# Six-stage decoder on one core: weights packed on the host and fetched a stage ahead, one preparation block, shifted rows fetched four batches at a time

## The chip, the cores and the metric

The kernel runs on one core of a Trainium2 chip. The time is the device time of one execution in microseconds (us); the number shown is the median of three runs. A profile is a separate execution, recorded by the hardware profiler, and it has its own time. The engines are PE (matrix products; PEld is its loading of weights), DVE, ACT and POOL (vector, activation and general work on SBUF), and SP, which here only issues DMAs.

## The reference: what is computed

The input is x, 64 batches of 128 tokens with 128 channels (f32), and a context of 64 batches of 77 rows with 64 channels. Two layers are applied, each of three blocks with a residual around it. `ln` is a layer norm without weights.

```python
x = x + linear_attention(ln(x))              # 16 heads of 8, random features, causal
x = x + cross_attention(ln(x), ctx)          # 16 heads of 64, 77 keys
x = x + local_transformer(ln(x))             # two layers, as below
x = x + mamba2(ln(x))                        # two directions, 4-tap convolution, scan over 128 tokens
x = x + context_attention(ln(x), ctx)        # 16 heads of 8
x = x + experts(ln(x))                       # 16 experts, top 2, silu

# one layer of the local transformer
h = shift_token(x)                           # channels 64..127 come from the token before, 0 for the first
q, k, v = split(h @ wqkv)                    # 8 heads of 64, normed, rotary position
x = x + local_attention(q, k, v) @ wo        # window of 64 tokens
h = layernorm(shift_token(x)) * ln_g + ln_b
a, g = split(h @ w1 + b1)                    # 341 columns each
x = x + (a * gelu(g)) @ w2 + b2
```

`shift_token` is the operation that a part of the change is about. Tokens lie on the 128 partitions, so to shift by a token is to move rows from partition p to p + 1. The kernel does it with two DMAs from SBUF to SBUF: channels 0 to 63 of 128 rows unmoved, and channels 64 to 127 of 127 rows moved down by one.

## The kernel before

The residual stream lives in SBUF (`k_x`, [128 tokens, 64 batches, 128 channels]). The stages run one after another. Each is one block with one instruction stream per engine, and each stream is a software pipeline over the 64 batches (`pipeline`, L99): step n of an engine's stream handles phase 0 of batch n, phase 1 of batch n-1 and so on, in an order that is written out by hand in its `step` function. Semaphores (`Stage`, L77) say which instruction of which batch another engine has finished. `at("c", b, ago=2)` is a wait for the instruction "c" of two batches back, as when a buffer of a pair is used again.

At the end of a stage `Memory.free` (L127) clears its semaphores and meets all engines at a barrier. SBUF buffers are allocated by stage, so nothing of a stage can be started before the last one is over. Each stage therefore begins with its weights' DMAs on SP's queue, small ones among them (one row spread over all partitions, one column), and the other engines wait on the semaphore `loaded` for all of them.

The stages, with the prefix of their names in the trace, are:

- constants (`k_`, L161), a block for POOL alone: identity, masks;
- linear attention (`la_`, L215): 30 weight DMAs, then x per batch;
- cross attention (`ca_`, L616), ahead of it a block `cw_` that loads four weight arrays, transposes them on PE and multiplies Wq with Wk and Wv with Wo head by head;
- local attention (`l_`, L996) and gated MLP (`m_`, L1345), twice. `lt_y` is the stream inside, `lt_hn` (`g.hn`) the shifted copy of it. Local attention's SP stream fetches the shifted rows of each batch for its own use (`l_h`, L1092 and L1093) and, once the batch's result is added to y, fetches the shifted rows of the result into `lt_hn` (L1083 and L1084). The block ends with SP waiting for all of these. POOL clears row 0 of `lt_hn` first (L1104). The gated MLP works on quads, four batches at a time: 16 quads in a pipeline of five phases, STAT, NORM, TURN, GATE, OUT. DVE takes statistics of the quad in `lt_hn` (L1549), POOL subtracts and scales (L1422, L1426), PE turns the quad into columns (L1513), DVE scales it into `m_hT` (L1567), and PE multiplies with w1 (L1484) and w2 (L1492);
- state model (`mb_`, L1587), ahead of it a block `mw_` that loads its arrays, multiplies the input projection with each of the four convolution taps on DVE, transposes and multiplies on PE;
- context attention (`xa_`, L2149) and experts (`mo_`, L2462). The experts' stage writes x out.

DVE's stream in the gated MLP matters for the prediction. In a step its phases come in the order STAT of quad n, GATE of quad n-3, OUT of quad n-4, TURN of quad n-2. So the first `m_hT`, that of quad 0, stands in step 2 behind the statistics of quad 2.

## Time and profile before

| | |
|---|---|
| time, median of 3 runs | 4214.08 us (4212.66 to 4217.06) |
| the profiled execution | 4216.15 us, span 4214.3 us |
| PE busy | 3899.9 us, 93% |
| PE's weight loads | 3022.5 us, 72% |
| DVE busy | 3020.9 us, 72% |
| ACT busy | 2842.6 us, 67% |
| POOL busy | 1818.1 us, 43% |
| TensorE clock granted, mean | 0.975 |

PE by fortieths of the span (a digit is the busy share in tenths, a slice is 105 us):

```profile
PE   6999799999979999788999986999999989998999
```

The span is that of all engines from the first instruction to the last; 1.85 us of the execution lie outside it. Where the digit falls to 6 or 7, two stages meet inside the slice, or (slices 12, 17 and 18) the local attention waits for other engines. In the timeline `SPq` is SP's queue of DMA issues; the length beside one is the issue, not the transfer. In the windows, "PEclk" is the share of full clock that was granted to TensorE in the stretch, "share" the mean busy share of the 16 DMA engines.

### The profile page before, as it was taken

The page shows a single profiled execution, that of the slowest core. Times are in us where ns is not written, and L with a number is a line of the kernel's source. Part 1 is how long each engine was busy: PE and PEld are TensorE (multiplying, and loading weights), DVE is VectorE, ACT ScalarE, POOL GpSimd, SP SyncE. Part 2 cuts the span into 40 slices and gives each one's busy share as a digit, 9 for nine tenths or more (in the row PEclk, how much of TensorE's full clock was granted, in tenths as well). Part 3 has the DMA queues.
Part 4 walks back from the last instruction along what each step waited for, and adds up shares of the span by engine and source line. Part 5 has one row for each costly group of instructions (what it writes and reads, how often), then busy time and mean ns, then how long its engine had stood idle before and what let it go on. Part 6 is the DMA issues. An engine that isn't in the chain of part 4 may idle for free. (4 is left out here: it accounts for less than half of the span.)

```text
span 4214.3 us, 107514 instructions
## 1 busy us (share of the span) xinstructions
PE 3899.9 (93%) x34047; PEld 3022.5 (72%) x34047; DVE 3020.9 (72%) x7623; ACT 2842.6 (67%) x6414; POOL 1818.1 (43%) x1728
## 2 busy tenths in 40 slices
PE   6999799999979999788999986999999989998999
PEld 4676678888746666675666675888888867776777
DVE  6888655555569999548999854777777757775665
ACT  5666455555569999648999963777777757774333
POOL 3333122222268888536777752333333321112443
PEclk9999899999989999999999998999999989999999
DMA  0000000000000000000000000000000000000000
GB/s 16 9 9 9 19 9 6 6 6 6 5 23 17 16 16 16 12 14 14 16 17 16 14 8 15 1 0 0 0 0 0 0 6 4 3 3 20 12 12 13
DMA packets 129425, 40.97 MB, mean 10 GB/s; under 512 B 104042, under 2 KB 128428, under 8 KB 129324
## 3 DMA queue, kind: packets, MB, share of 16 engines
q1 hardware_dynamic: 129324, 39.67, 4.0%
q8 instruction: 58, 0.95, 0.1%
q14 instruction: 43, 0.35, 0.0%
HBM read 18.72 MB, written 4.19 MB: 5 GB/s over the span
## 5 line engine op out<-in xcount | busy, mean ns | idle before, releaser
L1139 POOL TENSOR_TENSOR l_rc<-l_rc,l_rs 128x1024 f32<-128x1024 f32 x128 | 303.6, 2372 | 202.9 <-DVE l_rs L1332 201.2
L1206 ACT ACTIVATE l_prob<-l_prob,l_mx 128x128 f32<-128x128 f32 x1024 | 311.9, 389 | 0.0
L1824 POOL TENSOR_TENSOR mb_steps<-mb_upto,mb_dta 128x1024 f32<-128x1024 f32 x64 | 121.4, 1897 | 361.0 <-DVE mb_dta L2075 361.0
L780 POOL TENSOR_TENSOR ca_prob<-ca_prob,ca_sm 128x1232 f32<-128x1232 f32 x64 | 143.9, 2248 | 299.7 <-DVE ca_sm L946 299.7
L1231 PE MATMUL l_qk_ps<-l_wqkv,l_hT 128*128 128x512 f32 x512 | 248.6, 609 | 12.4 <-DVE l_rs L1332 10.4
L1133 POOL TENSOR_TENSOR l_prob<-l_prob,l_sm 128x1024 f32<-128x1024 f32 x128 | 242.8, 1897 | 17.1 <-DVE l_sm L1318 17.1
L1116 POOL TENSOR_TENSOR l_rc<-l_rc,l_ss 128x1024 f32<-128x1024 f32 x128 | 243.4, 1902 | 12.5 <-POOL l_rc L1139 4.5
L1976 PE MATMUL mb_x_ps<-mb_wx,mb_xT 128*128 128x256 f32 x1024 | 237.5, 386 | 0.0
L2548 POOL TENSOR_TENSOR mo_hid<-mo_hid,mo_gate 128x1024 f32<-128x1024 f32 x64 | 121.7, 1902 | 199.9 <-DVE mo_hid L2694 199.9
L1327 DVE TENSOR_REDUCE l_ss<-l_sq 128x16 f32<-128x1024 f32 x128 | 156.0, 1219 | 72.1 <-ACT l_sq L1170 71.8
L1976 PEld LDWEIGHTS mb_x_ps<-mb_wx,mb_xT 128*128 128x128 f32 x1024 | 190.8, 191 | 23.0
L1239 PEld LDWEIGHTS l_att_ps<-l_probT,l_val 128*64 128x64 f32 x2048 | 109.2, 136 | 127.4 <-ACT l_probT L1157 127.4
L2025 DVE SCALAR_TENSOR_TENSOR mb_pre<-mb_bc_ps,mb_cw,mb_pre 128x127 f32<-128x127 f32 (+2 forms) x576 | 193.1, 345 | 1.6 <-ACT mb_pre L1871 1.6
L807 ACT ACTIVATE ca_oT<-ca_go_ps 128x1024 f32<-128x1024 f32 x64 | 65.5, 1024 | 190.2 <-PE ca_go_ps L860 190.2
L1484 PE MATMUL m_ag_ps<-m_hT,m_w 128*128 128x256 f32 (+1 forms) x768 | 181.4, 388 | 1.9 <-DVE m_hT L1567 1.9
L2245 POOL TENSOR_TENSOR xa_kblock<-xa_kT,xa_gmask 128x308 f32<-128x308 f32 x64 | 44.8, 700 | 293.0 <-ACT xa_kT L2285 293.0
L1268 PEld LDWEIGHTS l_score_ps<-l_kT,l_qT 64*128 64x128 f32 x2048 | 124.6, 188 | 64.8 <-issue 51.7
L1296 DVE TENSOR_TENSOR l_prob<-l_score_ps,k_local 128x1024 f32<-128x1024 f32 x128 | 156.0, 1218 | 14.7 <-PE l_score_ps L1268 11.0
L1239 PE MATMUL l_att_ps<-l_probT,l_val 128*64 128x128 f32 x2048 | 140.1, 279 | 26.2 <-ACT l_probT L1157 9.7
L2579 ACT ACTIVATE mo_hidT<-mo_turn_ps 128x512 f32<-128x512 f32 x128 | 69.5, 594 | 139.6 <-PE mo_turn_ps L2623 139.6
L1315 DVE TENSOR_REDUCE l_sm<-l_prob 128x8 f32<-128x1024 f32 x128 | 155.5, 1215 | 8.1 <-ACT l_prob L1206 3.8
L958 DVE TENSOR_TENSOR k_x<-k_x,ca_y_ps 128x128 f32 (+1 forms) x64 | 18.4, 287 | 193.8 <-PE ca_y_ps L896 193.8
(377 smaller groups left out, 12208.5 us busy)
## 6 DMA issues: line engine op xcount, KB each, us to landing
la_xin<-in_x SPq DMA_DIRECT2D x64, 64.0 KB
l_h<-lt_y SPq DMA_DIRECT2D x128, 32.0 KB
lt_hn<-lt_y SPq DMA_DIRECT2D x128, 32.0 KB
out_x<-k_x SPq DMA_DIRECT2D x64, 64.0 KB, 1.5
l_h<-lt_y SPq DMA_DIRECT2D x128, 31.8 KB
lt_hn<-lt_y SPq DMA_DIRECT2D x128, 31.8 KB
ca_ctxT<-in_ctx_T SPq DMA_DIRECT2D x128, 19.2 KB, 2.0
l_wqkv<-in_L_ffn_wqkv SPq DMA_DIRECT2D x2, 768.0 KB
```

What stands on the lines that cost most here:

```text
L1116: gp.tensor_tensor(rc[l][:].rearrange("p a h e -> p (a h) e"), rc[l][:].rearrange("p a h e -> p (a h) e"), ss[l][:, 2].unsqueeze(2).to_bro ...
L1133: gp.tensor_tensor(heads, heads, sm[b.lane][:, 1].unsqueeze(2).to_broadcast([T, H, T]), ALU.mult).then_inc(*pool_prob.did("norm"))
L1139: gp.tensor_tensor(wide(rc[l][:]), wide(rc[l][:]), wide(rs[l][:]), ALU.add).then_inc(*pool_sum.did("rot"))
L1206: ex = sc.activation(p[:, a, j], p[:, a, j], ACT.Exp, bias=mx[l][:, a, j:j + 1])
L1231: mm = te.matmul(qk_ps[:, a], hT[b.slot][:], wqkv[:, a], start=True, stop=True)
L1239: mm = te.matmul(att_ps[HD * a:HD * a + HD, j], val[b.slot][:, 2 * j + a], probT[l][:, a, j], start=True, stop=True)
L1296: v.tensor_tensor(prob[b.slot][:].rearrange("p a j t -> p (a j) t"), score_ps[:].rearrange("p a j t -> p (a j) t"), g.local[:].unsqueeze(1 ...
L1315: v.tensor_reduce(sm[l][:, 0], prob[b.slot][:].rearrange("p a j t -> p (a j) t"), AX, ALU.add).then_inc(*vec_sum.did("sum"))
L1327: v.tensor_reduce(ss[l][:, 0], sq[l][:].rearrange("p a h e -> p (a h) e"), AX, ALU.add).then_inc(*vec_rot.did("ss"))
L1484: mm = te.matmul(ag_ps[half][0:M[c], c, N * a:N * a + N], w1[:, a, 128 * c:128 * c + M[c]], hT[b.lane][:, N * half:N * half + N], start=Tr ...
L1976: mm = te.matmul(x_ps[:, DI * k:DI * k + DI], xT[l][:, at_j:at_j + T], wx[:, k, j], start=(j == 0), stop=(j == TAPS - 1))
L2025: v.scalar_tensor_tensor(out=out, in0=bc_ps[:, T * i + there.start:T * i + there.stop], scalar=cw[:, k, 2 + SHIFTED[i][1], TAPS - 1 - back ...
```

## The change

Four things are changed.

*Packed weights.* The host lays the weights of each stage out as one array of 128 rows, with rows spread over partitions, columns and padding already in place (`laid_out`, `packed`). `Memory.weights` allocates the buffer and gives views by name. The sizes are 1284 columns for the linear attention (657 KB), 3072 for the cross attention, 2565 and 700 for the state model, 2304 and 1202 for each layer of local attention and gated MLP (1.80 MB a layer), 642 for the context attention and 3232 for the experts (1.98 MB together).

*Fetched a stage ahead.* These buffers outlive the stages, and one semaphore `g.fetched` counts all of them. SP issues the loads of the cross attention and the state model behind the last input of the linear attention, those of both local layers behind the last context of the cross attention, and those of the last two stages at the beginning of the state model. The constants are made by POOL inside the linear attention's block.

*One preparation block.* `prepare` stands between linear and cross attention and holds the work of `cw_` and `mw_`. ACT, not DVE, copies the cross products out of PSUM; POOL makes the scan's masks and the diagonal of D. The block `mw_` in front of the state model is gone.

*Shifted rows by quads.* `lt_hn` is gone. Local attention issues only its own fetches and waits for nothing at its end. The gated MLP's SP stream, empty before but for weights, fetches the shifted rows of a quad with two DMAs (128x4x64 and 127x4x64) into a pair of buffers `m_h`, in the phase STAT. A fetch waits until POOL has read the quad two back.

```diff
     def free(self):
-        self.nc.clear_and_free_semaphores(self.sems)
-        self.nc.all_engine_barrier()
+        if self.sems:
+            self.nc.clear_and_free_semaphores(self.sems)
+            self.nc.all_engine_barrier()
...
+    def weights(self, name, key):
+
+        buf = self.sb(name, [128, sum(width for _, width in PACKED[key])])
+        parts, start = {}, 0
+        for part, width in PACKED[key]:
+            parts[part] = buf[:, start:start + width]
+            start += width
+        return buf, parts
...
 # linear attention, SP
-                sp.dma_start(wqkv[:], d["L0_attn_Wqkv"]).then_inc(loaded, 16)
...
+                sp.dma_start(w[:], d["p_linear"]).then_inc(loaded, 16)
...
                 pipeline(sp, g.NB, LAST + 2, step, turn=4)
+                sp.dma_start(g.cross_w[:], d["p_cross"]).then_inc(g.fetched, 16)
+                sp.dma_start(g.state_w[:], d["p_state"]).then_inc(g.fetched, 16)
+                sp.dma_start(g.steps_w[:], d["p_steps"]).then_inc(g.fetched, 16)
+                sp.dma_start(g.cross_bo[:], row_bc(d["L0_xattn_bo"])).then_inc(g.fetched, 16)
...
 # cross attention, SP
                 pipeline(sp, g.NB, OUT + 1, step, turn=4)
+                for layer in (0, 1):
+                    sp.dma_start(g.local_w[layer][0][:], d["p_local"][layer]).then_inc(g.fetched, 16)
+                    sp.dma_start(g.gated_w[layer][0][:], d["p_gated"][layer]).then_inc(g.fetched, 16)
+                sp.dma_start(g.rot[:], d["rot"]).then_inc(g.fetched, 16)
...
 # local attention, SP
-                    b = at(OUT)
-                    if b:
...
-                        sp.wait_ge(*vec_y.at("y", b))
-                        sp.dma_start(to_low, low).then_inc(hn_in, 16)
-                        sp.dma_start(to_high, high).then_inc(hn_in, 16)
...
-                sp.wait_ge(hn_in, 32 * g.NB)
...
 # local attention, POOL
-                gp.memset(g.hn[0:1, :, HALF:C], 0.0).then_inc(zeroed, 1)
...
 # gated MLP, SP
                 sp.wait_ge(zeroed, NZERO)
-                sp.dma_start(lng[:], d["L0_ffn_ln_g"][layer].unsqueeze(1)).then_inc(loaded, 16)
...
+                def step(at):
+                    b = at(STAT)
+                    if b:
+                        index = b.index * Q if b.trip is None else sp.snap(b.index * Q)
+                        low = g.y[:, bass.ds(index, Q), 0:HALF]
+                        high = g.y[0:T - 1, bass.ds(index, Q), HALF:C]
+                        sp.wait_ge(*pool_norm.at("c", b, ago=2))
+                        sp.dma_start(h[b.lane][:, :, 0:HALF], low).then_inc(h_in[b.lane], 16)
+                        sp.dma_start(h[b.lane][1:T, :, HALF:C], high).then_inc(h_in[b.lane], 16)
+
+                pipeline(sp, g.NB // Q, OUT + 1, step)
...
 # gated MLP, POOL
                 for l in (0, 1):
+                    gp.memset(h[l][:], 0.0).then_inc(zeroed, 1)
...
-                        gp.tensor_tensor(off[l][:], quad(g.hn, b), mv[l][:, :, 0].unsqueeze(2).to_broadcast([T, Q, C]),
+                        gp.tensor_tensor(off[l][:], h[l][:], mv[l][:, :, 0].unsqueeze(2).to_broadcast([T, Q, C]),
...
 # gated MLP, DVE
+                        v.wait_ge(h_in[l], b.loaded(32))
                         for i in range(Q):
-                            v.bn_stats(stats[l][:, i], one(g.hn, b, i)).then_inc(*vec_stat.did(f"s{i}"))
+                            v.bn_stats(stats[l][:, i], h[l][:, i]).then_inc(*vec_stat.did(f"s{i}"))
```

The PE stream of the new block, with its own waits (`turned`, `copied`, `product`, `done` belong to the cross weights, `tap`, `across`, `kept` to the state model's):

```python
te.wait_ge(g.fetched, NFETCH)
for j in range(PAIRS):                      # 8 transposes of wq, then 16 of wk and wv
    mm = te.transpose(pc[:, j // 4, C * (j % 4):C * (j % 4) + C], wq[:, 128 * j:128 * j + 128], g.ident[:])
...
taps(0)                                     # 10 transposes of direction 0, tapped on DVE
te.wait_ge(copied, 3)
...                                         # 16 products for wqk
te.wait_ge(kept, NKEPT[0])
taps(1)                                     # 13 transposes of direction 1
...                                         # 16 products for wvo
```

Behind them come eight transposes and eight products for the state model's wz, wdt and wout.

The order of instructions at three places. On SP, where the cross attention ends and the local attention begins, there stand before (semaphores have the name that they were first given, so those of a later stage read `la_...`):

```order
92 L746 UNCONDITIONAL_BRANCH
93 L1059 UNCONDITIONAL_BRANCH [waits barrier_Pool_Activation_PE_DVE_SP_release]
94 L1061 DMA l_wqkv<-in_L_ffn_wqkv 128x1536
95 L1062 DMA l_wo<-in_L_ffn_wo 128x4x128
96 L1065 DMA l_qks<-in_L_ffn_q_scale 128x64
97 L1066 DMA l_qks<-in_L_ffn_q_scale 128x32
98 L1067 DMA l_qks<-in_L_ffn_q_scale 128x32
99 L1065 DMA l_qks<-in_L_ffn_k_scale 128x64
100 L1066 DMA l_qks<-in_L_ffn_k_scale 128x32
101 L1067 DMA l_qks<-in_L_ffn_k_scale 128x32
102 L1068 DMA l_rot<-in_rot 128x256
103 L1092 DMA l_h<-lt_y 128x64 [waits la_pe_last,la_zeroed]
```

And of the change:

```order
74 L680 DMA ca_ctx<-in_ctx 77x64 [waits la_act_feat] x4
75 L684 DMA w_local<-in_p_local 128x2304
76 L685 DMA w_gated<-in_p_gated 128x1202
77 L684 DMA w_local<-in_p_local 128x2304
78 L685 DMA w_gated<-in_p_gated 128x1202
79 L686 DMA w_rot<-in_rot 128x256
80 L662 UNCONDITIONAL_BRANCH
81 L1060 UNCONDITIONAL_BRANCH [waits barrier_Pool_Activation_PE_DVE_SP_release]
82 L1076 DMA l_h<-lt_y 128x64 [waits la_pe_score1,la_loaded]
```

The loads have moved across the barrier, into the cross attention's block, and hold for both layers; the first fetch of shifted rows is now the first thing that SP does in the local attention.

On DVE, in the first steps of the gated MLP, the statistics of quads 1 and 2 and the first `m_hT` stand before as:

```order
645 L1549 BN_STATS m_stats<-lt_hn 128x6 [waits la_act_keyT]
646 L1549 BN_STATS m_stats<-lt_hn 128x6 x3
647 L1551 MEMSET m_rstd 128x4 [waits la_prep]
648 L1553 BN_AGGR m_mv<-m_stats 128x2 x4
649 L1549 BN_STATS m_stats<-lt_hn 128x6 [waits la_act_keyT]
650 L1549 BN_STATS m_stats<-lt_hn 128x6 x3
651 L1551 MEMSET m_rstd 128x4 [waits la_prep]
652 L1553 BN_AGGR m_mv<-m_stats 128x2 x4
653 L1567 TENSOR_SCALAR m_hT<-m_turn_ps,m_lng,m_lnb 128x512 [waits la_act_turn,la_vec_last,la_loaded]
```

And of the change:

```order
657 L1532 BN_STATS m_stats<-m_h 128x6 [waits la_prep,la_act_keyT]
658 L1532 BN_STATS m_stats<-m_h 128x6 x3
659 L1534 MEMSET m_rstd 128x4 [waits la_made]
660 L1536 BN_AGGR m_mv<-m_stats 128x2 x4
661 L1532 BN_STATS m_stats<-m_h 128x6 [waits la_zeroed,la_act_keyT]
662 L1532 BN_STATS m_stats<-m_h 128x6 x3
663 L1534 MEMSET m_rstd 128x4 [waits la_made]
664 L1536 BN_AGGR m_mv<-m_stats 128x2 x4
665 L1547 TENSOR_SCALAR m_hT<-m_turn_ps,w_gated 128x512 [waits la_act_turn,la_vec_last]
```

The order is the same. Each group of statistics now has a second semaphore to wait for (`la_prep` and `la_zeroed` are the two lanes of `h_in`), that of the quad's fetch, and the first `m_hT` stands behind that of quad 2.

On SP the gated MLP's block of the change begins with

```order
130 L1373 UNCONDITIONAL_BRANCH [waits barrier_Pool_Activation_PE_DVE_SP_release]
131 L1384 DMA m_h<-lt_y 128x4x64 [waits la_act_keyT,la_loaded]
132 L1385 DMA m_h<-lt_y 127x4x64
133 L1384 DMA m_h<-lt_y 128x4x64 [waits la_act_keyT]
134 L1385 DMA m_h<-lt_y 127x4x64
135 L1384 DMA m_h<-lt_y 128x4x64 [waits la_act_keyT]
136 L1385 DMA m_h<-lt_y 127x4x64
```

where before it held the gated MLP's weights and no shifted rows.

## Rows read from the trace of the kernel before

**Rows 1.** windows: us, PE PEld DVE ACT POOL busy (x), PEclk, share, GB/s

```profile
0.00:23.05 23.05, 0.00 (x0) 0.00 (x1) 2.03 (x16) 3.56 (x7) 6.20 (x30) 1.00 0.14 30
...
501.45:528.05 26.60, 11.15 (x88) 10.11 (x88) 7.54 (x14) 1.78 (x3) 0.10 (x1) 0.58 0.24 62
...
1165.44:1182.88 17.44, 0.00 (x1) 0.00 (x0) 2.01 (x11) 2.17 (x5) 5.48 (x11) 0.57 0.29 82
...
1730.22:1743.80 13.58, 0.00 (x0) 0.01 (x1) 3.91 (x28) 6.59 (x9) 5.13 (x10) 0.66 0.22 49
...
1743.80:1882.51 138.71, 136.81 (x832) 119.97 (x832) 77.45 (x260) 80.64 (x152) 49.14 (x45) 0.97 0.00 0
...
1882.51:1893.60 11.09, 0.00 (x1) 0.02 (x1) 0.85 (x2) 1.28 (x1) 3.92 (x7) 0.60 0.45 128
...
2430.57:2444.30 13.73, 0.00 (x0) 0.02 (x1) 3.90 (x28) 6.75 (x9) 5.29 (x10) 0.63 0.24 49
...
2582.54:2624.70 42.16, 9.04 (x40) 7.55 (x40) 14.75 (x58) 2.69 (x7) 2.04 (x10) 0.60 0.17 37
...
3421.16:3431.87 10.71, 0.00 (x1) 0.03 (x1) 1.75 (x8) 2.45 (x6) 2.58 (x12) 0.63 0.15 35
```

**Rows 2.** timeline: start, us, engine line op out<-in xcount [idle before <-releaser]

```profile
17.26 0.17 DVE L527 TENSOR_SCALAR la_freq<-la_freq 128x2 f32<-128x2 f32 x1 [17.26 <-DMA la_omega<-in_L_attn_omega]
```

**Rows 3.** windows of the load ahead of the first weight block

```profile
504.00:506.00 2.00, 0.00 (x0) 0.00 (x0) 0.00 (x0) 0.00 (x0) 0.00 (x0) 0.50 0.94 338
...
508.00:510.00 2.00, 0.00 (x0) 0.00 (x0) 0.00 (x0) 0.00 (x0) 0.00 (x0) 0.50 0.89 205
```

**Rows 4.** timeline, first weight block

```profile
510.43 1.97 PE L656 MATMUL cw_pw<-k_ident,cw_wq 128*128 128x128 f32 x8 [8.99 <-DMA cw_wo<-in_L_xattn_Wo]
...
515.08 3.68 PE L667 MATMUL cw_pp<-cw_wkT,cw_wqT 64*128 64x64 f32 x32 [0.78 <-DVE cw_wvT L688]
```

**Rows 5.** timeline, opening of the state model's stage

```profile
2621.62 0.36 POOL L1799 MEMSET mb_xT<- 128x134 f32 x2 [35.71 <-POOLq L127]
```

**Rows 6.** timeline, end of cross-attention and start of local attention

```profile
1122.05 26.66 SPq L765 DMA_DIRECT2D ca_ctx<-in_ctx  x4
...
1166.61 0.36 SPq L1061 DMA_DIRECT2D l_wqkv<-in_L_ffn_wqkv  x1
...
1175.97 0.43 DVE L1287 TENSOR_TENSOR l_rot<-l_rot,l_qks 128x256 f32<-128x256 f32 x1 [10.21 <-DMA l_rot<-in_rot]
```

**Rows 7.** timeline, from local attention into the first gated stage

```profile
1731.15 0.65 SPq L1084 DMA_DIRECT2D lt_hn<-lt_y  x1
...
1735.57 0.10 POOL L1409 MEMSET m_eps<- 128x1 f32 x1 [10.47 <-POOLq L127]
...
1737.05 0.87 DVE L1549 BATCH_NORM_STATS2 m_stats<-lt_hn 128x6 f32<-128x128 f32 x4 [6.51 <-POOL m_gl L1413]
...
1745.00 0.81 DVE L1567 TENSOR_SCALAR m_hT<-m_turn_ps,m_lng,m_lnb 128x512 f32<-128x512 f32 x1 [2.53 <-issue]
...
1745.87 0.80 PE L1484 MATMUL m_ag_ps<-m_hT,m_w 128*128 128x256 f32 x1 [0.96 <-DVE m_hT L1567]
```

**Rows 8.** windows in which one hn half is in transfer (128 rows, 127 rows)

```profile
1731.75:1732.00 0.25, 0.00 (x0) 0.00 (x0) 0.00 (x0) 0.00 (x0) 0.00 (x0) 1.00 0.59 130
...
1732.75:1734.25 1.50, 0.00 (x0) 0.00 (x0) 0.00 (x0) 0.00 (x0) 0.00 (x0) 1.00 0.08 18
```

**Rows 9.** timeline, steady state of the first gated stage, DVE

```profile
1862.59 0.81 DVE L1567 TENSOR_SCALAR m_hT<-m_turn_ps,m_lng,m_lnb 128x512 f32<-128x512 f32 x1 [2.19 <-issue]
...
1870.88 0.81 DVE L1567 TENSOR_SCALAR m_hT<-m_turn_ps,m_lng,m_lnb 128x512 f32<-128x512 f32 x1 [2.18 <-issue]
```

**Rows 10.** timeline, second local layer, SP

```profile
1888.17 0.53 SPq L1092 DMA_DIRECT2D l_h<-lt_y  x1
```

**Rows 11.** timeline, starts of the last two stages, DVE

```profile
3430.12 0.18 DVE L2399 TENSOR_REDUCE xa_gmask<-xa_hmask 128x4 f32<-128x16 f32 x1 [7.66 <-DMA xa_bo<-in_L_xattn_bo]
...
3856.55 0.29 DVE L2648 BATCH_NORM_STATS2 mo_stats<-k_x 128x6 f32<-128x128 f32 x1 [10.03 <-DMA mo_b<-in_L_ffn_b]
```

More of the change, by code:

```diff
@@ L2710, in decoder @@
     with ExitStack() as scope:
[L2711 removed]
+        shared = Memory(nc, scope, "st")
+        g.stored, g.fetched = shared.sem("stored"), shared.sem("fetched")
+        g.NLOCAL, g.NLAST = 9 * 16, 11 * 16
         constants(nc, g, scope)
[L2713 to L2714 removed]
+        kept = Memory(nc, scope, "w")
+        g.rot = kept.sb("rot", [T, 2, 2, ROT_DIM])
+        g.local_w = [kept.weights(f"local{layer}", "local") for layer in (0, 1)]
+        g.gated_w = [kept.weights(f"gated{layer}", "gated") for layer in (0, 1)]
+        g.steps_w, g.steps_part = kept.weights("steps", "steps")
+        g.wx, g.wbc = kept.sb("wx", [C, 2, 4, 256]), kept.sb("wbc", [C, 2, 4, 2, 128])
+        g.wz, g.wdt, g.wout = kept.sb("wz", [C, 2, 2, 128]), kept.sb("wdt", [C, 8]), kept.sb("wout", [128, 2, 2, C])
+        g.ddiag = kept.sb("ddiag", [T, 8, T])
+        g.beyond, g.upto = kept.sb("beyond", [T, 2, T]), kept.sb("upto", [T, 2, T])
+        with ExitStack() as early:
+            cross = Memory(nc, early, "wc", "right")
+            g.wqk, g.wvo = cross.sb("wqk", [C, 8, 2, 64]), cross.sb("wvo", [128, 8, C])
+            g.cross_bo = cross.sb("bo", [T, C])
+            with ExitStack() as once:
+                raw = Memory(nc, once, "wr", "right")
+                g.cross_w, g.cross_part = raw.weights("cross", "cross")
+                g.state_w, g.state_part = raw.weights("state", "state")
+                linear_attention(nc, g)
+                prepare(nc, g)
+            cross_attention(nc, g)
+        local_transformer(nc, g)
+        with ExitStack() as late:
+            last = Memory(nc, late, "wl", "right")
+            g.context_w, g.context_part = last.weights("context", "context")
+            g.experts_w, g.experts_part = last.weights("experts", "experts")
+            mamba(nc, g)
+            context_attention(nc, g)
+            experts(nc, g)
 def kernel(**inputs):
@@ L2721 @@
     nc = bacc.Bacc("TRN2", target_bir_lowering=False, num_devices=1)
-    arrays = {name: np.ascontiguousarray(a) for name, a in inputs.items()}
+    arrays = {name: np.ascontiguousarray(inputs[name]) for name in ("x", "ctx_512", "L0_xattn_bo")}
     arrays.update(shape_tables())
```

684 lines of the change are left out of this document (326 added, 358 removed).

## The prediction

> **What bounds the kernel now.** The page's busy times come first: PE is the busiest engine by far. The windows by stage come next and say where it is not: inside a stage PE hardly stops (136.81 of 138.71 us in the first gated stage), but between stages it does nothing for 11 to 17 us, and at the start and around the two weight blocks the windows are 23, 27 and 42 us long [rows 1]. The change leaves the matmuls of the stages as they are, so its worth lies in these gaps. For each I look in the timeline for the wait that ends last, and for how far behind it PE's first instruction comes.
>
> **Start of the program.** DVE L527 waits until 17.26 for some 30 small loads [rows 2]; PE starts at 23.05 [rows 1], 5.8 later. Afterwards there is one load of 128x1284 numbers (657 KB), issued in the first microsecond. Bulk loads run at 205 to 338 GB/s [rows 3]: 1.9 to 3.2, and 1.4 to 2 from issue to transfer (the gated stage, below, shows 1.4): it lands at 3.9 to 6, I take 5.2. POOL's constants now lie inside the stage; all 30 POOL instructions of that window take 6.20 [rows 1], and I count 5.4 for those that are left ahead of the norm. PE then starts at 5.4 + 5.8 = 11.2: **-12** (-10 to -13).
>
> **First preparation block.** In the 26.60 us ahead of the cross-attention [rows 1] PE L656 waits 8.99 for the load [rows 4]. That goes: the arrays are asked for while the last batches of the linear attention run. In exchange the state model's products, until now a block of their own, are added. At the half clock of this window (0.58 granted [rows 1]) a transpose takes 1.97 / 8 = 0.246 and 32 passes of the products 3.68 [rows 4]. PE's row is then: 24 transposes for the cross weights 4.0 (eight of them, then sixteen with half the columns), taps of direction 0 (10) 2.5, 32 passes 3.7, taps of direction 1 (13) 3.2, 32 passes 3.7, 8 transposes 2.0, 8 products 2.0; 21.1 in all. Waits between engines add some 0.3 and DVE's last scaling 1.1. The state model's first matmul comes 3.1 behind its block's opening (2621.62 [rows 5] to 2624.70 [rows 1]), barrier included 3.8 behind the last instruction; here the chain is one norm shorter: 3.0. From 502.7 that is 502.7 + 21.1 + 1.4 + 3.0 = 528.2, no gain at half clock. With the clock up from the middle of the block (PE now works on without the copies' pauses) it is 5 less, at the full clock from the first transpose 8 less. I take **-3** (-8 to +1).
>
> **Cross-attention to the first local layer.** The cross-attention's last SP instruction is at 1122.05 + 26.66 = 1148.7, the next block opens at 1166.61 [rows 6]. In between now go 3.72 MB (two local, two gated arrays, the table): 11.0 to 18.2 at the rates of rows 3, so they land between 1161.1 and 1168.3, by the middle at 1164. DVE L1287, which waited until 1175.97 for nine loads [rows 6], goes at 1166.9. PE keeps its distance of 6.9 from it (its window ends at 1182.88 [rows 1]), since norm, fetch of h and landing lie between: 1173.85. **-9** (-7 to -9.1).
>
> **Inside local attention** two DMAs a batch and 3.5 us of POOL's fill go. SP isn't waited for in the body and PE's waits there don't name POOL's start: 0.
>
> **Into the gated stage.** Here is the change's price. Before, the last hn fetch is issued at 1731.15, POOL opens the block at 1735.57 once it has landed, DVE's statistics are at 1737.05, the first hT at 1745.00 and the first gate matmul at 1745.87 [rows 7]. DVE's last instruction of the layer ends at 1737.05 - 6.51 = 1730.54. Afterwards the block opens 0.8 behind it, 1731.4 (4.2 earlier), POOL fills for 2.1 (1.5 before), and SP issues the first quad's halves at 1733.5 and 1734.1. What does a quad cost? The old pair shows it: the 128-row half moves at share 0.59 and 130 GB/s, the 127-row half at share 0.08 and 18 GB/s, about one engine of 16 [rows 8]. The quad's 127x4x64 half has 130 KB, 7.2 to 7.4 at 18 GB/s, with the low half's share 7.8. All go through that one engine: with 1.4 to the start and 0.35 to the end's being seen they land at 1743.2, 1751.0, 1758.8, 1766.6. DVE's order puts the third quad's statistics ahead of the first hT (listing in the section on the change), so hT(0) waits until 1758.8 and four statistics (0.87), aggregates (0.4) and hT itself (0.8) follow: the first gate matmul at 1760.9, not 1745.87: **+15.0**.
> In the steady state PE takes a quad each 8.29 (1862.59 to 1870.88 [rows 9]) and the fetch 7.8: PE's body stays, with 0.5 to spare. A fetch waits until POOL has read the buffer of two quads back, some 4 behind that quad's landing and so well inside the 7.8 of the next: the engine doesn't run dry.
> Bounds of this term: if all 16 engines shared the half it would land 2.5 behind the issue; the third fetch is issued once POOL has read the first quad, at about 1741, and hT(0) comes at 1745.5: 0. If four engines shared it, +2.5. Above: 10 per quad would add 16 x 1.7 = 27, and 2.2 for each of three quads at the start.
> The Trainium skill ("DMA: Bandwidth & Descriptors", section "Why a DMA increments its semaphore by 16 and not by 1") has a rule for this: the hardware queue takes the largest number of engines up to 16 that divides the slowest dimension of both patterns, so 127 partitions go on one, 128 on all. The two shares agree with it. By that rule the four batches in the middle don't help, and it speaks against this change; if the whole count 127 x 4 decided, four engines would share the half and the term would be +2.5.
>
> **Second layer.** Into it: POOL and SP open at 1883.84 and SP reaches h's fetch at 1888.17 behind nine loads [rows 10]; now 0.7 after the opening. PE's 1893.60 [rows 1] becomes about 1888.7: **-4.9** (-4 to -5.5; SP no longer waits for the queue either). Its own gated stage has the same waits and the same shape: **+14.9**.
>
> **Into the state model.** Of 42.16 us [rows 1], loads and products last until POOL L1799 at 2621.62 [rows 5]; both go. The block opens at 2583.9 and PE comes 3.1 behind it, 2587.1: **-37.6** (-36 to -40).
>
> **Last two stages.** DVE L2399 comes at 3430.12 after an idle of 7.66, for loads alone [rows 11]; POOL's masks let it go at 3426.05: **-4.1**. DVE L2648 comes at 3856.55 after 10.03 idle [rows 11]; with no load it comes 1.2 after the last stage's end, -8.8, and 0.3 comes back since ACT's table load of 1.28 is then on the way: **-8.5**.
>
> **Sum.** -12 - 3 - 9 + 15.0 - 4.9 + 14.9 - 37.6 - 4.1 - 8.5 = -49.2. Against the profiled execution's own 4216.15 us that is 4167.0. It ran 2.07 over the median shown (4214.08), so the median should be 4165.
>
> **The rivals.**
> (A) The quad's high half spreads over several engines. Then the two +15 become 0 to +2.5 each: 4165 - 25 = 4140, to 4135. For it: the trace holds no transfer of 127 rows with a middle dimension. Against it: the steady 0.08 of the flat one. 15%.
> (B) The one engine bounds the gated stages. If a quad needs D, not 7.8, the bodies cost 32 x (D - 8.29) and the starts 6 x (D - 7.8) more. D = 9 gives 4165 + 23 + 7 = 4195; D = 10 gives 4233. It turns into a loss from D = 9.5 (49 given back). For it: 0.5 is a margin of 6%, and the 508 rows of 256 B wait behind the low half's share on the same engine. Against it: 18 GB/s is a measured mean over that very kind of row. D of 8.4 to 9.4: 10%; above: 4%.
> (C) The weights don't come in the shadow: at 205 GB/s they land 1.7 late, or the bulk holds back the last batches' inputs. It costs up to 9 at that place, 4174. 8%.
> (D) The clock rises sooner, since PE's pauses are shorter: it was granted 0.50 to 0.66 in all the gaps [rows 1]. That would be 3 to 8 more: 4159. 15%.
> (E) The change doesn't do what it says: early loads wait for memory still in use, and the old waits come back (12 + 9 + 5 + 4 + 8, and 16 of the 38), 4219. The listing shows the loads behind SP's last fetch with no wait: 2%.
>
> **How the numbers follow.** The forecast itself 46%, (C) and (D) beside it 23%, (A) 15%, (B) 14%, (E) 2%. The range goes from 4136, which takes in most of (A), to 4190, the middle of the mild (B). A difference under 0.2% (8.4 us) can't be told from none here: 4205.7 to 4222.5. Slower by more than that needs D over 9.7: 4%. Same: 9.3 to 9.7, or (E): 3%. Faster: 93%.
>
> **What would show it.** In the new profile: DVE's first la_freq near 5, PE's first matmul near 11; in the cross weights' block PE busy for about 20 us; local attention's rot product within 0.4 of its block's opening; in each gated stage DVE idle some 7 us ahead of each of the first three statistics of m_h, released by the DMA m_h, with the DMA share near 0.07, and hT steps of 8.3 afterwards. Wrong, if the DMA share in that start-up is above 0.2 and DVE's idle under 3 us (then A); if hT steps exceed 8.4 with DVE waiting for m_h (then B); if local attention's first DVE instruction waits for w_rot (then C).

## The result and the profile after

The changed kernel takes 4175.61 us (median of 4 runs, 4174.64 to 4176.52), the kernel before 4215.57 on the same chips (4212.66 to 4218.63): ratio 0.9905, 95% interval 0.9888 to 0.9922. That is 40 us less; 49 were forecast. It is faster, inside the range of 4136 to 4190 and 10.6 above the point.

The profiled execution spans 4174.8 us (before 4214.3). These windows go from the start of PE's last row in one stage to the start of its first in the next (the two gated starts end at the first gate matmul). The columns are those of [rows 1].

```profile
488.63:513.65 25.02, 17.46 (x129) 15.04 (x130) 14.83 (x48) 7.54 (x14) 3.54 (x8) 0.72 0.01 2
...
1150.76:1161.05 10.29, 2.05 (x16) 1.89 (x17) 2.01 (x11) 2.17 (x5) 2.04 (x10) 0.71 0.05 10
...
1706.34:1738.15 31.81, 2.24 (x12) 1.68 (x12) 4.71 (x29) 8.08 (x12) 7.34 (x13) 0.58 0.13 30
1738.15:1877.13 138.98, 135.10 (x816) 118.72 (x816) 76.48 (x259) 79.03 (x149) 44.78 (x43) 0.97 0.10 24
1877.13:1884.77 7.64, 1.61 (x13) 1.45 (x13) 0.85 (x2) 1.28 (x1) 0.48 (x6) 0.82 0.07 15
...
2420.63:2452.38 31.75, 2.25 (x12) 1.68 (x12) 4.72 (x29) 8.08 (x12) 8.60 (x14) 0.57 0.13 30
2452.38:2592.63 140.25, 135.98 (x816) 119.36 (x816) 76.43 (x259) 79.03 (x149) 63.78 (x58) 0.96 0.10 24
2592.63:2599.27 6.64, 1.60 (x12) 1.45 (x13) 1.80 (x8) 2.28 (x5) 0.46 (x4) 0.97 0.43 143
```

And the same two stretches of the first gated stage in the kernel before:

```profile
1729.06:1745.87 16.81, 2.25 (x13) 1.68 (x13) 4.77 (x30) 8.59 (x12) 7.20 (x12) 0.66 0.18 40
1745.87:1880.91 135.04, 134.12 (x817) 117.85 (x817) 76.58 (x259) 78.63 (x149) 47.07 (x43) 0.98 0.00 0
```

The way to the first gate matmul has grown by the 15.0 of the prediction (31.81 less 16.81). But the rest of the stage has grown too, 138.98 against 135.04, and that was forecast as 0. All stretches between the same PE rows, in us:

| stretch | before | after | difference | forecast |
|---|---|---|---|---|
| to PE's first matmul | 23.08 | 10.81 | -12.3 | -12 |
| linear to cross attention | 27.13 | 25.02 | -2.1 | -3 |
| cross attention to local | 19.52 | 10.29 | -9.2 | -9 |
| first gated MLP, from local's last PE row to its own | 151.85 | 170.79 | **+18.9** | +15.0 |
| gated to second local | 12.70 | 7.64 | -5.1 | -4.9 |
| second gated MLP | 151.53 | 172.00 | **+20.5** | +14.9 |
| gated to state model | 43.76 | 6.64 | -37.1 | -37.6 |
| state model to context attention | 11.32 | 7.36 | -4.0 | -4.1 |
| context attention to experts | 12.78 | 4.27 | -8.5 | -8.5 |
| bodies: linear, cross, both local, state, context, experts | | | -0.1, +1.8, -0.9, +0.1, +2.2, -3.1, -0.7 | 0 |

The sum is -39.5 where -49.2 was forecast. Of the 9.7 us between them 9.5 are in the gated stages. The start of the first one, timeline of the changed kernel (start, length, engine, line, what is written from what, idle before and its releaser):

```profile
1706.34 1.16 PE L1260 MATMUL l_v_ps<-w_local,l_attT 128*128 128x128 f32 x8 [0.70 <-ACT l_attT L1157]
...
1711.48 0.77 SPq L1385 DMA_DIRECT2D m_h<-lt_y  x1
...
1720.86 0.87 DVE L1532 BATCH_NORM_STATS2 m_stats<-m_h 128x6 f32<-128x128 f32 x4 [13.04 <-DMA m_h<-lt_y]
...
1728.48 0.87 DVE L1532 BATCH_NORM_STATS2 m_stats<-m_h 128x6 f32<-128x128 f32 x4 [6.32 <-DMA m_h<-lt_y]
...
1736.11 0.87 DVE L1532 BATCH_NORM_STATS2 m_stats<-m_h 128x6 f32<-128x128 f32 x4 [6.35 <-DMA m_h<-lt_y]
...
1737.32 0.78 DVE L1547 TENSOR_SCALAR m_hT<-m_turn_ps,w_gated 128x512 f32<-128x512 f32 x1
...
1738.15 7.40 PE L1465 MATMUL m_ag_ps<-m_hT,w_gated 128*128 128x256 f32 x24 [11.78 <-DVE m_hT L1547]
...
1743.77 0.87 DVE L1532 BATCH_NORM_STATS2 m_stats<-m_h 128x6 f32<-128x128 f32 x4 [5.67 <-DMA m_h<-lt_y]
...
1746.94 2.27 ACT L1433 ACTIVATE m_gl<-m_ag_ps,w_gated 128x256 f32<-128x256 f32 x6
1747.53 1.26 DVE L1514 SCALAR_TENSOR_TENSOR m_u<-m_ag_ps,w_gated,m_gl 128x256 f32<-128x256 f32 x3 [2.47 <-ACT m_gl L1433]
...
1748.94 2.88 PE L1473 MATMUL m_o_ps<-w_gated,m_u 128*128 128x128 f32 x12 [2.96 <-DVE m_u L1514]
```

In the kernel before, the first m_u and the w2 matmuls that read it (m_o) stand at:

```profile
1752.07 1.26 DVE L1532 SCALAR_TENSOR_TENSOR m_u<-m_ag_ps,m_b,m_gl 128x256 f32<-128x256 f32 x3 [5.06 <-ACT m_gl L1450]
...
1754.35 1.50 PE L1492 MATMUL m_o_ps<-m_w,m_u 128*128 128x128 f32 x12
```

The statistics of the first three quads come 7.6 apart, each released by its fetch (7.8 were forecast), and hT(0) follows the third, as the order of DVE says. Then the fourth quad's come at 1743.77. They stand, on DVE and on ACT, ahead of the GATE work of quad 0 (ACT's gelu, `m_gl`, and DVE's product with it, `m_u`), so m_gl comes at 1746.94 and m_u at 1747.53, and PE waits 2.96 for it. This fourth landing isn't in the prediction's sum. While the first quad's halves are in transfer, the trace of the changed kernel shows the low half (first window) and the high half behind it (second):

```profile
1712.00:1712.50 0.50, 0.00 (x0) 0.00 (x0) 0.00 (x0) 0.01 (x1) 0.00 (x0) 0.50 0.72 175
...
1714.00:1718.00 4.00, 0.00 (x0) 0.00 (x0) 0.00 (x0) 0.00 (x0) 0.00 (x0) 0.50 0.08 18
```

That is the 0.08 and 18 GB/s of [rows 8], now held for several us. The share alone doesn't count the engines (0.08 of 16 would be 1.3); that it is one is argued, from the two experiments on the rows below.

### The profile page after: what moved, and what is told of

Same layout as the page of the kernel before. It is cut to its first block and busy times, and to the rows that moved or that the text cites. A ratio compares the mean times of both kernels' runs of the same rounds, so it can differ in the third digit from the quotient of the medians.

```text
span 4174.8 us, 106854 instructions
## 1 busy us (share of the span) xinstructions
PE 3893.2 (93%) x34047; PEld 3016.7 (72%) x34047; DVE 3014.2 (72%) x7607; ACT 2847.6 (68%) x6423; POOL 1804.9 (43%) x1724
## 5 line engine op out<-in xcount | busy, mean ns | idle before, releaser
L1840 POOL TENSOR_TENSOR mb_steps<-w_upto,mb_dta 128x1024 f32<-128x1024 f32 x64 | 121.4, 1896 | 363.2 <-DVE mb_dta L2092 363.2
L1213 PE MATMUL l_qk_ps<-w_local,l_hT 128*128 128x512 f32 x512 | 248.5, 609 | 13.2 <-DVE l_rs L1313 10.9
L1993 PE MATMUL mb_x_ps<-w_wx,mb_xT 128*128 128x256 f32 x1024 | 237.1, 385 | 0.0
L1993 PEld LDWEIGHTS mb_x_ps<-w_wx,mb_xT 128*128 128x128 f32 x1024 | 190.1, 191 | 23.3
L1465 PE MATMUL m_ag_ps<-m_hT,w_gated 128*128 128x256 f32 (+1 forms) x768 | 181.8, 388 | 23.6 <-DVE m_hT L1547 23.6
L2042 DVE SCALAR_TENSOR_TENSOR mb_pre<-mb_bc_ps,w_steps,mb_pre 128x127 f32<-128x127 f32 (+2 forms) x576 | 192.8, 343 | 1.6 <-ACT mb_pre L1888 1.6
L1465 PEld LDWEIGHTS m_ag_ps<-m_hT,w_gated 128*128 128x128 f32 (+1 forms) x768 | 135.9, 184 | 49.6 <-DVE m_hT L1547 24.4
## 6 DMA issues: line engine op xcount, KB each, us to landing
l_h<-lt_y SPq DMA_DIRECT2D x128, 31.8 KB
```

The source lines that it names most:

```text
L1213: mm = te.matmul(qk_ps[:, a], hT[b.slot][:], wqkv[:, a], start=True, stop=True)
L1465: mm = te.matmul(ag_ps[half][0:M[c], c, N * a:N * a + N], w1[:, a, 128 * c:128 * c + M[c]], hT[b.lane][:, N * half:N * half + N], start=Tr ...
L1993: mm = te.matmul(x_ps[:, DI * k:DI * k + DI], xT[l][:, at_j:at_j + T], wx[:, k, j], start=(j == 0), stop=(j == TAPS - 1))
L2042: v.scalar_tensor_tensor(out=out, in0=bc_ps[:, T * i + there.start:T * i + there.stop], scalar=cw[:, k, 2 + SHIFTED[i][1], TAPS - 1 - back ...
```

## Experiments

The runs were made against the kernel before on the same chips. Against the changed kernel they are compared by medians; the kernel before had medians of 4212.6 to 4215.8 in the four sets, so a difference of a few us between sets says nothing. For places inside, times are counted from the start of local attention's last PE row (L1260 in the changed kernel), which I call "the end of local".

**The number of engines: 112 and 15 rows**

```diff
-                        sp.dma_start(h[b.lane][1:T, :, HALF:C], high).then_inc(h_in[b.lane], 16)
+                        sp.dma_start(h[b.lane][1:113, :, HALF:C], high[0:112]).then_inc(h_in[b.lane], 16)
+                        sp.dma_start(h[b.lane][113:T, :, HALF:C], high[112:T - 1]).then_inc(h_in[b.lane], 16)
```

> The quad's high half goes as two DMAs, 112 rows and 15 rows, in place of one of 127 rows; nothing else differs from the changed kernel. Theory 1 (one engine carries the 127-row half): the landings of the first quads come 2 to 3 us apart and not 7.6; a quad is then paced by the reading of its buffer. The first gate matmul comes 16 to 17 us after local attention's last PE row and not 31.8, the gated stages lose their start-up cost, -15 to -19 us each: 4137 to 4146 in all. Rival 2 (the half is slow because it has 508 short rows, or because one SBUF-to-SBUF transfer shifts partitions, however many engines take part): the split changes nothing, 4174 to 4177, landings 7.6 apart.

Measured: 4138.00 us (4137.12 to 4139.22), ratio to the kernel before 0.9816 (0.9799 to 0.9832). The gated stages take 151.05 and 151.39, less than before the change (151.85 and 151.53). First statistics and first hT, timeline of this kernel:

```profile
1714.37 0.87 DVE L1533 BATCH_NORM_STATS2 m_stats<-m_h 128x6 f32<-128x128 f32 x4 [6.75 <-DMA m_h<-lt_y]
...
1722.31 0.78 DVE L1548 TENSOR_SCALAR m_hT<-m_turn_ps,w_gated 128x512 f32<-128x512 f32 x1
```

Theory 1 holds, and the rival is out: one extra DMA a quad, 0.9 to 1.0 us of SP's queue, takes away 37.6 us, at the near end of the 4137 to 4146 that it gave.

**Is it the split, or the rows? 122 and 5 rows**

```diff
-                        sp.dma_start(h[b.lane][1:113, :, HALF:C], high[0:112]).then_inc(h_in[b.lane], 16)
-                        sp.dma_start(h[b.lane][113:T, :, HALF:C], high[112:T - 1]).then_inc(h_in[b.lane], 16)
+                        sp.dma_start(h[b.lane][1:123, :, HALF:C], high[0:122]).then_inc(h_in[b.lane], 16)
+                        sp.dma_start(h[b.lane][123:T, :, HALF:C], high[122:T - 1]).then_inc(h_in[b.lane], 16)
```

> The quad's high half goes as 122 rows and 5 rows. It has as many DMAs as the split into 112 and 15 (4138.0), so it tells whether the split as such counts or the number of rows. Theory 1 (the largest number of engines up to 16 that divides the rows carries them: 2 for 122, 16 for 112): a quad takes 7.2 x 122 / 127 / 2 + 0.4 = 3.9, the first statistics come 3 to 4 earlier than in the changed kernel, the DMA share in that transfer is about 0.12 to 0.13, and the whole 4146 to 4153. Rival 2 (two DMAs in place of one is all that counts): 4136 to 4141, as with 112 and 15. Rival (122 rows still sit on one engine): 4173 to 4177.

Measured: 4149.50 (4145.32 to 4149.89), ratio 0.9848 (0.9830 to 0.9865), inside theory 1's 4146 to 4153. Window while the 122 rows are in transfer:

```profile
1712.00:1712.80 0.80, 0.00 (x0) 0.00 (x0) 0.00 (x0) 0.00 (x0) 0.00 (x0) 0.50 0.15 32
```

Share and rate are nearly twice those of 127 rows (0.08, 18). The first statistics come 11.2 after the end of local, against 14.5 with 127 rows and 8.2 with 112. The number of rows decides, not the split as such. The Trainium skill has a rule for it ("DMA: Bandwidth & Descriptors", section "Why a DMA increments its semaphore by 16 and not by 1"): a DMA is carried by the largest number of engines up to 16 that divides its slowest dimension, which is 1 for 127 rows, 2 for 122 and 16 for 112 or 128. The traces agree with it in three shapes, with 18, 32 and, for the old 128-row half, 130 GB/s.

**What the fetch's slack is: a fifth batch**

```diff
                         sp.dma_start(h[b.lane][1:T, :, HALF:C], high).then_inc(h_in[b.lane], 16)
+                        sp.dma_start(spare[b.lane][1:T, :], high[:, 0]).then_inc(h_in[b.lane], 16)
```

> Each quad's fetch gets a fifth batch's high half in addition (127x64 into a spare buffer that nothing reads), so one more batch's worth of one-engine transfer. It measures the slack of the steady state. Theory 1 with the fetch at 7.6 a quad and 1.85 for the fifth: 9.4 to 9.5 a quad against PE's 8.3, the steps of hT become 9.4, each gated stage 16 x 1.1 to 1.2 = 18 to 19 longer plus 4 x 1.85 at the start: 4225 to 4231, slower than the kernel before. Rival (the fetch has more slack than it seems, since landings at 7.6 are paced by the reading of buffers and not by the engine): steps stay at 8.3 and only the start grows, under 4190.

Measured: 4213.56 (4211.80 to 4217.30), ratio 0.9995 (0.9985 to 1.0005). The whole gain of the change is gone. DVE in the steady state of its first gated stage:

```profile
1833.71 0.87 DVE L1534 BATCH_NORM_STATS2 m_stats<-m_h 128x6 f32<-128x128 f32 x4 [1.61 <-DMA m_spare<-lt_y]
1838.98 0.80 DVE L1549 TENSOR_SCALAR m_hT<-m_turn_ps,w_gated 128x512 f32<-128x512 f32 x1
1843.21 0.87 DVE L1534 BATCH_NORM_STATS2 m_stats<-m_h 128x6 f32<-128x128 f32 x4 [1.66 <-DMA m_spare<-lt_y]
1848.49 0.80 DVE L1549 TENSOR_SCALAR m_hT<-m_turn_ps,w_gated 128x512 f32<-128x512 f32 x1
```

Steps are 9.4 and 9.5 in turn and DVE waits for the DMA in each, so in the steady state it is the transfer that sets the pace, as expected. The time was expected 11 to 17 higher: I had added the start's 4 x 1.85 to all 16 steps, but the start's quads are among the 16. The stages grew by 19.4 and 18.2, in the first 5.4 of it up to the first gate matmul and 14.0 behind it, about 12 steps' worth. So rival (B) of the prediction was near. The fetch takes 7.6; from 8.3 on, 9% more, it would bound the stage, and at 9.4 to 9.5, 25% more, nothing is left of the gain.

**Which quad sets the start: TURN ahead of STAT**

```diff
                 def step(at):
+                    b = at(TURN)
+                    if b:
+                        v.wait_ge(*pe_turn.at("hT", b))
...
                     b = at(STAT)
                     if b:
                         l = b.lane
```

> On DVE in the gated MLP the phase TURN (hT of quad n-2) is put ahead of STAT (statistics of quad n). Theory T, the prediction's: hT(0) behind the statistics of quad 2 is what costs the start; with it ahead the first gate matmul comes near 1727 and each gated stage gains 8 to 11 us: 4154 to 4160. Theory F: the start is set by the fourth quad, since DVE's and ACT's GATE of quad 0 stand behind their STAT of quad 3 (landing 1743.8), so the first m_u stays at about 1747.5; the gate matmul comes early and PE then waits longer: 4173 to 4178.

Measured: 4395.95 (4393.54 to 4398.03), ratio 1.0425 (1.0408 to 1.0442). Neither theory had that number, but the start tells them apart:

```profile
1705.94 1.16 PE L1260 MATMUL l_v_ps<-w_local,l_attT 128*128 128x128 f32 x8 [0.70 <-ACT l_attT L1157]
...
1730.12 7.81 PE L1465 MATMUL m_ag_ps<-m_hT,w_gated 128*128 128x256 f32 x24 [4.14 <-DVE m_hT L1530]
...
1747.13 2.44 DVE L1514 SCALAR_TENSOR_TENSOR m_u<-m_ag_ps,w_gated,m_gl 128x256 f32<-128x256 f32 x6 [2.47 <-ACT m_gl L1433]
1748.54 2.90 PE L1473 MATMUL m_o_ps<-w_gated,m_u 128*128 128x128 f32 x12 [10.17 <-DVE m_u L1514]
```

The first gate matmul comes 7.6 earlier than in the changed kernel (24.2 after the end of local, not 31.8), and the first m_u no earlier: 41.19 after the end of local in both. PE's wait has only moved, from ahead of the gate matmul to behind it (10.17). Theory F holds. The 220 us come from the steady state: with TURN first DVE stands still for PE's turn, which PE does behind both gate halves of the older quad:

```profile
1809.45 0.81 DVE L1530 TENSOR_SCALAR m_hT<-m_turn_ps,w_gated 128x512 f32<-128x512 f32 x1 [6.80 <-PE m_turn_ps L1494]
...
1815.64 2.92 PE L1473 MATMUL m_o_ps<-w_gated,m_u 128*128 128x128 f32 x12 [6.23 <-DVE lt_y L1521]
...
1826.56 0.81 DVE L1530 TENSOR_SCALAR m_hT<-m_turn_ps,w_gated 128x512 f32<-128x512 f32 x1 [7.33 <-PE m_turn_ps L1494]
```

A step is 17.0 to 17.1 in place of 8.3. That I hadn't seen in the order.

**STAT last on DVE and ACT**

```diff
+                    b = at(GATE)
+                    if b:
+                        for half in (0, 1):
+                            gate(b, half)
                     b = at(STAT)
                     if b:
                         l = b.lane
                         sc.preload_act_table_set("natural_log_exp_and_others")
...
-                    b = at(GATE)
-                    if b:
-                        for half in (0, 1):
-                            gate(b, half)
```

(on ACT; on DVE the phase STAT is moved behind the second half of GATE in the same way)

> On DVE and on ACT in the gated MLP the phase STAT is put last in a step, behind TURN and GATE. Theory F (the fourth quad's statistics ahead of quad 0's GATE set the start): the first m_u follows the third quad's statistics (1736.1) and comes near 1738 to 1740 in place of 1747.5, each stage gains 6 to 9 us if the last quads don't give it back: 4158 to 4164. Theory T alone (only hT(0) behind quad 2 counts): hT(0) also comes early here, gain 8 to 11 a stage. Rival 3: with statistics last the way from landing to hT is a phase longer, and PE waits in the steady state: hT steps over 8.3, slower than 4176.

Measured: 4162.07 (4158.09 to 4163.37), ratio 0.9869 (0.9853 to 0.9885). The first m_u comes 33.55 after the end of local (1741.05 less 1707.50) in place of 41.19: 7.6 less, one landing. The stages take 163.17 and 163.07, 7.6 and 8.9 less than in the changed kernel. With one quad fewer ahead of GATE(0) the start costs one transfer fewer, and the steady state keeps its 8.3. This run alone doesn't tell the theories apart, since the first gate matmul too comes 7.6 earlier here (24.2 after the end of local); together with TURN ahead of STAT, where the gate matmul moved alone and the m_u stayed, it does.

**The first two quads fetched by local attention**

```diff
+                sp.wait_ge(*vec_y.at("y", Batch(7)))
+                for n in (0, 1):
+                    sp.dma_start(g.h[n][:, :, 0:HALF], g.y[:, 4 * n:4 * n + 4, 0:HALF]).then_inc(g.h_in[layer][n], 16)
+                    sp.dma_start(g.h[n][1:128, :, HALF:C], g.y[0:127, 4 * n:4 * n + 4, HALF:C]).then_inc(g.h_in[layer][n], 16)
```

(the pair `m_h` lives outside the stage here, under the name `lt_h`, and POOL clears it in the first local attention, not in the gated block)

> The shifted rows of the first two quads of each gated MLP are fetched by local attention's SP stream behind its last own fetch, while the attention still computes; the transfers keep their shape (127 rows on one engine), the others stay where they are. Theory F (what counts is how late the fourth quad lands): quads 2 and 3 are asked for when quads 0 and 1 have been read, 5 and 8 us after the block opens, and land at 7.6 apart from then on, so the fourth lands some 13 earlier than in the changed kernel: 4148 to 4154. If the start of each stage stayed DMA-paced all through (rival: the prefetch only moves the wait), over 4165.

Measured: 4148.01 (4144.77 to 4151.33), ratio 0.9845 (0.9829 to 0.9862), at the lower edge of theory F's 4148 to 4154. The gated stages take 157.42 and 155.95, 13.4 and 16 less than in the changed kernel. The fourth quad's statistics and the first m_u of its first gated stage:

```profile
1728.00 0.87 DVE L1538 BATCH_NORM_STATS2 m_stats<-lt_h 128x6 f32<-128x128 f32 x4 [5.66 <-DMA lt_h<-lt_y]
...
1731.76 1.26 DVE L1520 SCALAR_TENSOR_TENSOR m_u<-m_ag_ps,w_gated,m_gl 128x256 f32<-128x256 f32 x3 [2.47 <-ACT m_gl L1439]
```

Counted from the end of local (1703.74) they come at 24.3 and 28.0, where the changed kernel has 37.4 and 41.2: both 13.2 earlier. The first m_u has moved with the fourth landing for a second time.

**Prefetch and split together**

```diff
+                    sp.dma_start(g.h[n][1:113, :, HALF:C], g.y[0:112, 4 * n:4 * n + 4, HALF:C]).then_inc(g.h_in[layer][n], 16)
+                    sp.dma_start(g.h[n][113:128, :, HALF:C], g.y[112:127, 4 * n:4 * n + 4, HALF:C]).then_inc(g.h_in[layer][n], 16)
```

(in place of the last line of the edit above, with the split of the first experiment for the later quads)

> As in the run with the prefetch, and each high half is split into 112 and 15 rows as well. Theory 1: nothing in the gated stages waits for a fetch any more; against the split alone (4138.0) the wait of 6.8 us ahead of the first statistics falls to about 1.5: 10 us less, 4127 to 4130. Rival (the start is then set by something else, ACT's table loads or POOL's passes): 4133 to 4138.

Measured: 4127.42 (4126.73 to 4128.99), ratio 0.9794 (0.9778 to 0.9811): 48 us faster than the changed kernel, in theory 1's range, and with the next run the fastest of all. The stages take 145.95 and 147.41, 4 to 6 less than before the change. One premise of the expectation didn't come true: the first statistics no longer wait for a fetch, but those of the third quad, whose rows are asked for in the gated block, do:

```profile
1717.15 0.87 DVE L1540 BATCH_NORM_STATS2 m_stats<-lt_h 128x6 f32<-128x128 f32 x4 [4.36 <-DMA lt_h<-lt_y]
```

**Local attention's own fetch split as well**

```diff
-                        sp.dma_start(h[b.lane][1:T, HALF:C], high).then_inc(h_in[b.lane], 16)
+                        sp.dma_start(h[b.lane][1:113, HALF:C], high[0:112]).then_inc(h_in[b.lane], 16)
+                        sp.dma_start(h[b.lane][113:T, HALF:C], high[112:T - 1]).then_inc(h_in[b.lane], 16)
```

> The version with prefetch and split (4127.4), and local attention's own fetch of 127 rows is split into 112 and 15 rows too. Its body is not paced by it (one PE wait of 8.2 at the start, none later), so only the two starts gain, up to 1.5 each less the extra issue of 0.6: 4124 to 4127. Rival (the third DMA a batch delays SP or the landings in the body): 4128 to 4135.

Measured: 4127.43 (4126.22 to 4131.60), ratio 0.9798 (0.9780 to 0.9815): nothing gained. The two starts get 0.8 and 0.9 shorter (10.45 to 9.63, 7.70 to 6.84), and the local bodies 1.8 and 1.5 longer (545.34 to 547.10, 536.28 to 537.82). The runs that leave local attention as it is in the changed kernel have bodies of up to 546.7 and 537.5, so whether that is the third DMA a batch, as the rival has it, or chance isn't told apart.

**The weights at the start of local attention**

```diff
 # cross attention, SP, behind its pipeline: the five loads taken out
-                for layer in (0, 1):
-                    sp.dma_start(g.local_w[layer][0][:], d["p_local"][layer]).then_inc(g.fetched, 16)
...
 # first local attention, SP, at its start
+                if layer == 0:
+                    for i in (0, 1):
+                        sp.dma_start(g.local_w[i][0][:], d["p_local"][i]).then_inc(g.fetched, 16)
```

> The five packed loads of the local transformer (3.72 MB) are issued by SP at the start of the first local attention, not behind the last input of the cross attention; nothing else differs from the changed kernel. Theory (fetching them a stage ahead is what the -9 of this gap is made of): 3.72 MB at 205 to 338 GB/s need 11 to 18 us, DVE's first instruction waits for them and PE follows 6.9 behind, so PE's first matmul comes 12 to 18 later than in the changed kernel: 4188 to 4194. Rival (packing nine small loads into few is what counts, the early issue little): under 4180.

Measured: 4186.74 (4185.52 to 4189.72), ratio 0.9935 (0.9918 to 0.9951). The gap is 21.62 in place of 10.29, +11.3, just under the expected 12 to 18, since DVE had the arrays 11.4 after the first issue:

```profile
1153.30 0.36 SPq L1060 DMA_DIRECT2D w_local<-in_p_local  x1
...
1164.75 0.42 DVE L1269 TENSOR_TENSOR l_rot<-w_rot,w_local 128x256 f32<-128x256 f32 x1 [12.28 <-DMA w_rot<-in_rot]
```

The loads ran faster than the 205 to 338 GB/s that the prediction and this expectation took from [rows 3]:

```profile
1160.00:1162.00 2.00, 0.00 (x0) 0.00 (x0) 0.00 (x0) 0.00 (x0) 0.00 (x0) 0.50 0.99 418
```

The gap is 2.1 longer than before the change (19.52), so the -9 needs the early issue. What packing alone is worth isn't shown: the late load holds both layers' arrays and the gated MLP's, 3.72 MB, where before only one layer's local arrays stood there, and a packed load of those alone was not run.

**Two preparation blocks**

```diff
                 linear_attention(nc, g)
-                prepare(nc, g)
+                prepare_cross(nc, g)
...
         local_transformer(nc, g)
+        prepare_state(nc, g)
```

> The one preparation block is cut in two: the cross weights' products stay ahead of the cross attention, the state model's get a block of their own ahead of the state model, as before, but with their arrays already in SBUF. Theory (the two shares of the block run beside each other only in part, PE being busy 17.5 of 25.0 us in it): the first gap gets 7 shorter (PE's row loses 11 but waits for copies more), the second 21 longer (from the first tapped product to the state model's first matmul it was 24.5 with loads done, less 3 for what is common): 4186 to 4191. Rival (merging gains nothing, the products cost the same wherever they stand, and only the loads counted): 4176 to 4179.

Measured: 4187.62 (4184.58 to 4190.05), ratio 0.9940 (0.9923 to 0.9956), 12.0 more than the changed kernel. Both gaps of this kernel:

```profile
488.48:506.19 17.71, 10.45 (x90) 9.36 (x91) 1.24 (x6) 7.08 (x12) 0.10 (x1) 0.67 0.01 2
2582.14:2609.84 27.70, 11.40 (x52) 9.18 (x52) 15.17 (x50) 3.98 (x8) 4.06 (x11) 0.59 0.10 33
```

The first is 7.3 shorter, the second 21.1 longer than in the changed kernel, as expected. Of the -37.1 into the state model and the -2.1 ahead of the cross attention, 14 come from the products standing in one block. The other 25 are what both versions have over the kernel before: loads that no longer lie in the gaps, and copies and masks moved to ACT and POOL. These weren't separated.

## Why the prediction was right, and where it was short

- Start of the program: right (-12.3 for -12). DVE's scaling of the frequencies (L517, now a part of `la_w`) is at 4.85, PE's first matmul at 10.81; 5.8 between them became 6.0.
- First preparation block: -2.1 for -3, PE busy 17.5 of 25.0. The -3 was chosen between 0 at half clock and -8 at full clock, so its closeness isn't owed to the sum. How much the clock gives varies from run to run: of the ten profiles in which this block is the same, PE's part took 14.8 to 15.3 in three, at a granted clock of 0.79 to 0.89, and 17.7 to 17.8 in seven, at 0.64 to 0.67; the end of the block moved with it. In those three the gap is 22.0 to 22.5, that is -4.6 to -5.1. It is rival (D), with 2 more than forecast, and not each time.
- Cross to local attention: -9.2 for -9. That it hangs on the early issue is shown by the late weights.
- Into the second layer, the state model and the last two stages: -5.1, -37.1, -4.0 and -8.5 for -4.9, -37.6, -4.1 and -8.5.
- The gated stages: the mechanism was right up to the first gate matmul, +15.0 and +14.9 forecast and +15.0 and +14.8 measured. That the first is met to the tenth is luck in part: the first statistics came 0.4 later than the sum has it, and the two spacings behind them were 7.6 each, not 7.8. The step that failed is "hT(0) waits until 1758.8 ... the first gate matmul at 1760.9: +15.0", taken as the whole term. I stopped at the third quad, where hT(0) stands, and took the body behind it as PE's, 0 longer. The phase GATE of quad 0 stands behind the statistics of a fourth quad on both DVE and ACT. The first m_u came 23.0 after the end of local before (1752.07 less 1729.06) and 41.19 after: +18.2 of the stage's +18.9. TURN ahead of STAT moved the gate matmul and left the first m_u where it was; STAT last took one landing away and 7.6 with it; the prefetch brought the fourth landing 13.2 earlier, and the first m_u with it. So the term stops one landing short: it should have gone on to the fourth, and is too small by 3.9 in the first layer. In the second it is too small by 5.6, of which 1.3 and 0.5 have the cause given two items below.
- What the 3.9 are made of: the first w2 matmul comes 10.8 behind the first gate matmul, not 8.5, and behind the wait PE runs at a lower clock. The w2 matmuls took 2.88 and the gate matmuls next to them 3.14, where 1.50 and 2.76 are full clock. Windows of these two in the first layer, and of the gate matmuls in the second:

```profile
1748.94:1751.62 2.68, 2.67 (x13) 2.68 (x13) 1.75 (x4) 1.56 (x2) 0.00 (x0) 0.51 0.30 70
1751.62:1754.76 3.14, 3.14 (x15) 2.60 (x15) 1.58 (x10) 1.12 (x3) 0.56 (x1) 0.88 0.08 18
...
2465.85:2470.25 4.40, 4.40 (x15) 3.44 (x15) 1.58 (x10) 1.78 (x3) 1.04 (x1) 0.62 0.08 18
```

- In the second layer the body is 1.3 longer than in the first (140.25 and 138.98), and that is the clock again, 4.40 for the gate matmuls behind the wait and not 3.14. It doesn't belong to the second layer. In the run with the late weights, whose gated stages are those of the changed kernel, it fell on the first (bodies 140.19 and 138.95). Another 0.5 lies in the kernel before, whose second body is that much shorter than its first (134.58 and 135.04). The late weights' first layer:

```profile
1762.27 4.35 PE L1466 MATMUL m_ag_ps<-m_hT,w_gated 128*128 128x256 f32 x12
```

- The steady state of the gated stage: right. hT steps are 8.30 from the fourth hT on, and the margin of 0.7 (8.3 less 7.6) was as thin as rival (B) said. (B)'s price was too high: it takes 8.29 from all 32 quads and counts the starts beside them. For the 9.45 of the fifth batch its formula gives 47, and the run cost 38.
- Rival (A) is out: the middle dimension of 4 brings no second engine, the rate is the 18 GB/s of the flat rows. (C) is out: local attention's rot product comes at 1154.01 behind the barrier (idle 0.87, released by PE at L128), not behind a load. (E) is out, as no stretch of the table has its old wait back.
- The bodies: of cross (+1.8) and context attention (-3.1) kernels that don't differ there show as much (635.63 to 637.73 and 410.29 to 413.63), so it is not put down to the change. The state model's +2.2 is steadier: 795.85 before, 797.6 to 798.4 in nine of the ten kernels with one preparation block (794.8 in the one with TURN first), 795.02 with two blocks. It grows evenly, with batches 12.37 and 12.40 to 12.45 apart in turn, not 12.25 and 12.45, at an equal busy time of PE. Its cause was not tried and stays open.
